# A two-layer graph network on one core: of every 64 gathered chunks, SyncE and ScalarE each load one row by row

## The reference

```python
def _gcn_conv(x, W, b, src, dst, n):
    h = x @ W
    deg = segment_sum(ones, dst)
    dinv = where(deg > 0, rsqrt(deg), 0)
    msgs = h[src] * (dinv[src] * dinv[dst])[:, None]
    return segment_sum(msgs, dst) + b

h = maximum(_layernorm(x), 0)
h = h @ W_pre + b_pre
h = relu(_gcn_conv(h, W1, b1, src + loops, dst + loops, n))
h = relu(_gcn_conv(h, W2, b2, src + loops, dst + loops, n))
x = x + (h @ W_post + b_post)
h = maximum(_layernorm(x), 0)
x = x + attention(h)
```

## Time and profile before

| | us |
|---|---|
| median of 3 runs | 4922.3 |
| lowest, highest run | 4919.2, 4923.6 |
| the profiled execution's own time | 4947.8 |
| its span, from the first to the last instruction | 4945.9 |
| POOL busy, share of the span | 62% |
| PE, PEld busy | 57%, 42% |
| DVE, ACT busy | 27%, 8% |

### The profile page before, as it was taken

How to read it: one execution, slowest core, us unless ns; L and a number is a source line. 1 busy time by engine, 2 the same in 40 slices (tenths; PEclk the granted TensorE clock), 3 DMA queues, 4 the chain that set the end, 5 groups by cost and what they waited for, 6 DMA issues and landing times.

```text
span 4945.9 us, 31104 instructions
## 1 busy us (share of the span) xinstructions
PE 2821.1 (57%) x10330; PEld 2094.8 (42%) x10330; DVE 1321.9 (27%) x3053; ACT 380.4 (8%) x1154; POOL 3056.4 (62%) x3240
## 2 busy tenths in 40 slices
PE   3266565665656656566635667655555555555543
PEld 2144444444434444444424446534344443443432
DVE  8211111121211112111112323223232232322345
ACT  2110000000000000000100000000000000000000
POOL 0466666666666666666366666666666666666552
PEclk8577676777767777677767766677676776766666
DMA  6433333333333333333233434344343443444334
GB/s 186 121 103 106 104 106 103 106 106 106 105 103 106 105 107 105 103 106 103 77 94 110 110 106 108 107 114 110 104 114 107 113 110 104 113 109 111 98 91 127
DMA packets 294666, 534.91 MB, mean 108 GB/s; under 512 B 76792, under 2 KB 194472, under 8 KB 294504
## 3 DMA queue, kind: packets, MB, share of 16 engines
q0 software_dynamic: 153184, 413.34, 31.3%
q1 hardware_dynamic: 141320, 119.55, 8.1%
HBM read 480.91 MB, written 51.74 MB: 108 GB/s over the span
## 4 chain that ended last, share of the span: by engine, by line
PE 37%; issue 30%; another core or an unknown queue 22%; DVE 10%; ACT 1%; POOL 0%; DMA 0%; DVEq 0%; ACTq 0%; POOLq 0%
PE ps L1098 26%; PE ps L937 3%; PE ps L1033 3%; PE ps L1034 2%; DVE acc L1655 2%; DVE sel L1482 1%; PE ps L931 1%; DVE xin L1491 1%; DVE sel L1346 1%; DVE acc L1510 1%; DVE xin L1336 1%; DVE tsb L1508 0%; DVE stats L1512 0%; PE ps L1061 0%
## 5 line engine op out<-in xcount | busy, mean ns | idle before, releaser
L633 POOL DMA_INDIRECT big<-tab,idx x3126 | 2955.9, 946 | 1721.2 <-issue 1067.2
L1098 PE MATMUL ps<-big,sel 128*128 128x257 f32 (+1 forms) x6252 | 2084.5, 463 | 1112.8 <-issue 1093.0
L1098 PEld LDWEIGHTS ps<-big,sel 128*128 128x128 f32 x6252 | 1405.7, 232 | 1644.2 <-issue 1456.6
L1655 DVE SCALAR_TENSOR_TENSOR acc<-ps,here,acc 128x257 f32<-128x257 f32 (+1 forms) x392 | 190.1, 485 | 3417.6 <-remote 2934.0
L1482 DVE TENSOR_TENSOR sel<-rel,ps 128x1024 f32<-128x1024 f32 x392 | 474.4, 1211 | 0.0
L1033 PE MATMUL ps<-xin,Wc 128*128 128x128 f32 x784 | 167.8, 313 | 186.9 <-issue 183.9
L1033 PEld LDWEIGHTS ps<-xin,Wc 128*128 128x128 f32 x784 | 133.5, 211 | 207.6 <-issue 190.1
L937 PE MATMUL ps<-Wp,xin 128*128 128x256 f32 x392 | 132.0, 469 | 106.7 <-DVEq L1511 84.3
L1655 DVE SCALAR_TENSOR_TENSOR acc<-ps,beyond,acc 128x257 f32<-128x257 f32 (+1 forms) x392 | 186.6, 476 | 0.0
L1034 PE MATMUL ps<-xin,bc_row 1*128 1x128 f32 x392 | 113.9, 352 | 124.0 <-issue 123.6
L931 PE MATMUL ps<-ident,xin 128*128 128x128 f32 x392 | 95.7, 319 | 94.9 <-issue 82.8
(11 more groups left out here) (182 smaller groups left out, 1364.0 us busy)
## 6 DMA issues: line engine op xcount, KB each, us to landing
big<-tab,idx POOLq DMA_INDIRECT x3126
tab<-big SPq DMA_DIRECT2D x14, 910.0 KB, 5.5
acc<-tab SPq DMA_DIRECT2D x98, 130.0 KB
tab<-tsb SPq DMA_DIRECT2D x98, 128.0 KB
acc<-tab SPq DMA_DIRECT2D x98, 128.0 KB
xres<-acc SPq DMA_DIRECT2D x98, 128.0 KB
xin<-in_x_dram SPq DMA_DIRECT2D x97, 128.0 KB
big<-in_x_dram SPq DMA_DIRECT2D x13, 896.0 KB, 8.5
```

The costliest lines, as they stand in the source:

```text
L633: return pool.indirect_dma_start(out=to, out_offset=None, in_=table, in_offset=bass.IndirectOffsetOnAxis(ap=index, axis=0))
L1098: ins = pe.matmul(sums[H % SUMS][:, 0:n_c], sel[:, H % RING * CPH + j, :], G[:, H % PORTIONS * CPG + j, 0:n_c], start=(j == 0), stop=(j == ...
L1655: dve.scalar_tensor_tensor(out=row(T, wide), in0=sums[H % SUMS][:, 0:wide], scalar=mask[:, n:n + 1], in1=row(T, wide), op0=ALU.mult, op1=A ...
```

## The change

Every eighth half (n = 8k + 7, for k from 1 to 23 in each layer, `piece(n)` gives k) has its last two chunks, j = 6 and 7, loaded without a gather. SP loads the rows of chunk 6, ScalarE those of chunk 7, each row with a DMA of its own, into `hrow`, which has two places for each of the two. Four tiles share the 128 rows of a piece, so each engine issues 32 in a tile (`share`). SP first loads the piece's edge sources into `hidx` (`next_indices`); VectorE multiplies them by the row's bytes (`row_offsets` of VectorE, one instruction a piece), and each engine reads 32 of the products at once into registers. TensorE waits before each of the two chunks until the piece's loads have landed (`fed`), and takes the chunk from `hrow`.

```diff
+PERIOD = 4
...
+        hrow = sb("hrow", [P, 2, 2, W])
+        hidx = sb("hidx", [1, 3, 2, P], I32)
...
+        PIECES = FULL // (PERIOD * CPI) - 1
+        def piece(n):
+            k = (n + 1) // (2 * PERIOD) - 1
+            return k if (n + 1) % (2 * PERIOD) == 0 and 1 <= k <= PIECES else 0
+        def feeder(n, j):
+            return j - (CPG - 2) if piece(n) and j >= CPG - 2 else None
...
+        def share(m):
+            return m * P // PERIOD, (m + 1) * P // PERIOD
...
+            def row_loads(c, t):
+                k, m = t // PERIOD + 1, t % PERIOD
+                K = k + c * PIECES
+                if k > PIECES:
+                    return
+                if m == 0:
+                    n = c * HALVES + (k - 1) * 2 * PERIOD
+                    if n:
+                        sp.wait_ge(g_agg, n)
+                    next_indices(c, k)
+                    sp.wait_ge(h_off, K)
+                lo, hi = share(m)
+                _, at = nc.values_load_multi_w_load_instructions(
+                    hidx[0:1, K % 3, 0, lo:hi], engines=[mybir.EngineType.SP], min_val=0, max_val=(N - 1) * 4 * width(c),
+                    skip_runtime_bounds_check_because="indices of edges are node numbers")
+                for e in range(lo, hi):
+                    sp.dma_start(hrow[e:e + 1, K % 2, 0, 0:width(c)].bitcast(U8),
+                                 offset_of(at[e - lo], tab2 if c else tab1, width(c))).then_inc(hs_in[K % 2], 16)
...
                     if t >= 2:
                         store_tab2(t - 2)
+                    row_loads(0, t)
...
                         sp.wait_ge(c2_h, t + 1)
                         load_self(1, t + AR)
+                    row_loads(1, t)
...
                         for j in range(min(CPG, C - n * CPG)):
+                            if feeder(n, j) is not None:
+                                continue
                             gather(G[:, s * CPG + j, 0:width(c)], table, idx[:, n * CPG + j:n * CPG + j + 1]).then_inc(g_in[s], 16)
...
                 for i in range(ITERS - 3):
+                    at = row_offsets(0, i)
+                    row_loads(0, i, at, 0, 4)
                     for n in (2 * i, 2 * i + 1):
                         selT_copy(n, 0)
...
                     if due(i - 3):
                         root(i - 3)
+                    at = row_offsets(1, i)
+                    row_loads(1, i, at, 0, 3)
                     if due(i - 5):
                         values_out(i - 5)
                     if due(i - 4):
                         normed_turned(i - 4)
+                    row_loads(1, i, at, 3, 4)
...
+                x_j = G[:, H % PORTIONS * CPG + j, 0:n_c]
+                k, feed = piece(n), feeder(n, j)
+                K = k + c * PIECES
+                if feed == 0:
+                    pe.wait_ge(hs_in[K % 2], fed(c, k))
+                if feed == 1:
+                    pe.wait_ge(ha_in[K % 2], fed(c, k))
+                if feed is not None:
+                    x_j = hrow[:, K % 2, feed, 0:n_c]
...
+                    dve.wait_ge(h_idx, 32 * K)
+                    dve.tensor_scalar(hidx[:, K % 3, :, :], hidx[:, K % 3, :, :], 4 * width(c or k == PIECES), None, ALU.mult)\
+                       .then_inc(h_off, 1)
```

More of the change, by code:

```diff
@@ L16 @@
 I32 = mybir.dt.int32
+U8 = mybir.dt.uint8
 ALU = mybir.AluOpType
@@ L295, in build_gnn @@
         g_sel = sem("g_sel")
+        h_idx = sem("h_idx")
+        h_off = sem("h_off")
+        hs_in = [sem("hs_in0"), sem("hs_in1")]
+        ha_in = [sem("ha_in0"), sem("ha_in1")]
         a_in = [sem(f"a_in{s}") for s in range(AR)]
@@ L358, in build_gnn, with first_edge, fed, offset_of @@
         whole = FULL // P * P
+        PIECES = FULL // (PERIOD * CPI) - 1
+        assert (N - 1) * 4 * W < 1 << 24 and PIECES * PERIOD + 2 < ITERS - 3
+        def piece(n):
[3 more added lines that the diff above has]
+            return j - (CPG - 2) if piece(n) and j >= CPG - 2 else None
+        def first_edge(k, feed):
+            return ((k + 1) * PERIOD * CPI - 2 + feed) * P
+        def fed(c, k):
+            K = k + c * PIECES
+            return 16 * P * ((K + 1) // 2)
+        def share(m):
+            return m * P // PERIOD, (m + 1) * P // PERIOD
+        def offset_of(at, table, n):
+            return table.rearrange("n w -> (n w)").bitcast(U8)[bass.ds(at, 4 * n)].rearrange("(a b) -> a b", a=1)
         def landed(H):
-            return 16 * sum(min(CPG, C - n % HALVES * CPG) for n in range(H % PORTIONS, H + 1, PORTIONS))
+            return 16 * sum(min(CPG, C - n % HALVES * CPG) - 2 * (piece(n % HALVES) > 0)
+                            for n in range(H % PORTIONS, H + 1, PORTIONS))
         def cols(t):
@@ L506, in load_self, with next_indices @@
                 sp.dma_start(row(T, width(c)), (tab2 if c else tab1)[cols(t), :]).then_inc(a_in[s], 16)
+            def next_indices(c, k):
+                K = k + c * PIECES + 1
+                if K <= 2 * PIECES:
+                    for feed in range(2):
+                        at = first_edge((K - 1) % PIECES + 1, feed)
+                        sp.dma_start(hidx[0:1, K % 3, feed, :], src[at:at + P].rearrange("(a e) -> a e", a=1)).then_inc(h_idx, 16)
+            def row_loads(c, t):
[16 more added lines that the diff above has]
+                                 offset_of(at[e - lo], tab2 if c else tab1, width(c))).then_inc(hs_in[K % 2], 16)
             for s in range(XB):
@@ L510, in _ @@
             with sp.If(bad == 0):
+                next_indices(0, 0)
                 for t in range(AR):
@@ L828, in general_attention, with row_offsets, row_loads @@
                     exps(BATCHES - 2 + q)
+            def row_offsets(c, i):
+                k, m = (i - 1) // PERIOD + 1, (i - 1) % PERIOD
+                K = k + c * PIECES
+                if not 1 <= k <= PIECES:
+                    return ()
+                if m == 0:
+                    n = c * HALVES + (k - 1) * 2 * PERIOD
+                    if n:
+                        act.wait_ge(g_agg, n)
+                    if c and k == 1:
+                        for s in range(2):
+                            act.wait_ge(c1_w[s], 16 * (TILES // 2 + 1))
+                    act.wait_ge(h_off, K)
+                lo, hi = share(m)
+                _, at = nc.values_load_multi_w_load_instructions(
+                    hidx[0:1, K % 3, 1, lo:hi], engines=[mybir.EngineType.Activation], min_val=0, max_val=(N - 1) * 4 * width(c),
+                    skip_runtime_bounds_check_because="indices of edges are node numbers")
+                return at
+            def row_loads(c, i, at, first, end):
+                k, m = (i - 1) // PERIOD + 1, (i - 1) % PERIOD
+                K = k + c * PIECES
+                for q in range(first * len(at) // 4, end * len(at) // 4):
+                    e = share(m)[0] + q
+                    act.dma_start(hrow[e:e + 1, K % 2, 1, 0:width(c)].bitcast(U8),
+                                  offset_of(at[q], tab2 if c else tab1, width(c))).then_inc(ha_in[K % 2], 16)
             bad = act.value_load(flag_i[0:1, 0:1], min_val=0, max_val=1)
@@ L1097, in chunk @@
                     return
-                ins = pe.matmul(sums[H % SUMS][:, 0:n_c], sel[:, H % RING * CPH + j, :], G[:, H % PORTIONS * CPG + j, 0:n_c],
+                x_j = G[:, H % PORTIONS * CPG + j, 0:n_c]
+                k, feed = piece(n), feeder(n, j)
+                K = k + c * PIECES
+                if feed == 0:
[4 more added lines that the diff above has]
+                    x_j = hrow[:, K % 2, feed, 0:n_c]
+                ins = pe.matmul(sums[H % SUMS][:, 0:n_c], sel[:, H % RING * CPH + j, :], x_j,
                                 start=(j == 0), stop=(j == last))
@@ L1484, in select, with row_offsets @@
                                   iota_p.unsqueeze(1).to_broadcast([P, CPH, P]), ALU.is_equal).then_inc(g_sel, 1)
+            def row_offsets(c, i):
+                k = i // PERIOD
+                K = k + c * PIECES + 1
+                if i % PERIOD == 0 and k <= PIECES and K <= 2 * PIECES and (k or not c):
+                    dve.wait_ge(h_idx, 32 * K)
+                    dve.tensor_scalar(hidx[:, K % 3, :, :], hidx[:, K % 3, :, :], 4 * width(c or k == PIECES), None, ALU.mult)\
+                       .then_inc(h_off, 1)
             def rows(c, t, b, before):
```

2 lines of the change are left out of this document (added).

## The result

The changed kernel takes 6302.2 us (median; 6295.6 to 6315.5), beside 4922.9 us for the kernel before, measured beside it: 1.281 times as long, with a 95% interval of 1.279 to 1.282. The forecast was 5029 us, with a range up to 5290. It is slower, as forecast, but by 1380 us and not by 107. The profiled execution took 6295.6 us.

A forecast was written before the change was run, and what follows sets the result against it. POOL's own time was 30.0 of each 34.3 us cycle, TensorE's bursts deciding its restart. Layer 1 gaining 57 and layer 2 losing 165 gave +107 us: 5029 us for the median, range 4800 to 5290.

The forecast's parts named there:

- p: Price of a one-row DMA on SP or ScalarE: taken as 0.30 us, bounds 0.27 and 0.47.
- T + 32p = 10.6 us a tile: Time SP or ScalarE spends per tile on one register read and 32 row loads; taken as covered in layer 1.
- T: One read of 32 registers on SP or ScalarE: taken as 1.0 us, between 0.5 and 2.0.
- B: Rival: SP and ScalarE become the bound at 22.8 us a tile, 24.4 with ScalarE's work; 5675 us, chance 0.07.
- The gathers removed: On POOL, both layers: 92 gathers fewer at 1.25 us each save 115 us.
- rival C: Landing of gathers, not POOL's issue, sets the 1.43 us a chunk, so no gain: 4922 us, chance 0.05.
- Layer 1 gains 57: In layer 1 the row loads are hidden and the removed gathers make the layer 57 us shorter.
- SP's store ahead of the rows in layer 2: SP's last row loads stand behind store_l in their tile of use: 222 us lost, layer 2 net 165 longer.
- A: Rival: all row loading is hidden and only the removed gathers count; 4807 us, or 4791 with waits, chance 0.28.
- What costs nothing: VectorE's 46 multiplications, the DMA engines' at most 376,832 packets, and the waits for h_off and g_agg were taken as free.
- D: Layer 2, from the even half's end to the odd one's: 8.8 + 2T + 56p = 27.6 us, against 8.6 before.
- the three places of POOL's cycle: Where the even half ends after POOL's restart: at 0, 3.0 or 11.7 us, losing 16.2, 7.7 or 5.0; 9.6 a piece.

The follow-up runs named there:

- a layer without rows: Changed kernel with no row loads, register reads or waits for them: 4793.5 us on a slow-paced chip, 4156.3 us on a quick one, ratio 0.974 on both.
- the rows first: Changed kernel with SP's row loads ahead of store_l and load_self in layer 2: 5893.0 us slow-paced (1.197), 4154.9 us quick (0.973).
- experiment 3: Changed kernel with one line moved, so SP loads rows before store_l and load_self in layer 2: 4154.9 and 4154.8 us on quick chips, ratio 0.973.
- rows loaded for nobody: Changed kernel with all gathers made and used again, the rows still loaded but TensorE not waiting for them: 4267.4 us on a quick chip, ratio 0.9995.
- The fixed rows: Changed kernel with each row DMA from a fixed row, no register read or MOVE: 4226.5 and 4228.7 us quick, 5238.2 us slow-paced (1.064).
- the share of 64 half rows: Changed kernel with each row loaded by two DMAs of half a row, and semaphores for each layer: 6597.0 us on a quick chip, ratio 1.545.

## Why the prediction was wrong

**Where the 1380 us lie**, by the windows. Against 2159 us a layer without rows, layer 1 loses 533 us and layer 2 loses 524 with the rows first (2692, 2683): that is the price of the shares. SP's order in layer 2 adds 3082 - 2683 = 399. The gathers give back 129. The sum is 1327. Of the 53 us that are missing, 34 lie between and behind the layers; the rest is about the precision of a sum over several chips and executions.

**What failed is the price of a row**, p = 0.30 with bounds of 0.27 and 0.47, and the T + 32p = 10.6 us a tile that follows, and with them the step that such a tile is covered by POOL's 22.8 us in layer 1. Measured on SP in layer 1 were 24.2/32 = 0.76 us a row and 24.2 + 2.1 = 26.3 us a tile; from one share to the next it was 28.5 us on average. The price was taken from L395, issued before POOL gathers at all, and from medians. A median over a nearly idle queue says little about a full one where the pace depends on what else runs. The trace had a sign of it twice: L506 had a maximum of 1478 ns beside its median of 378, and TensorE executed eight matmul records in 16 us without a wait, which I read as TensorE's affair. Such stretches cost SP nothing while it issued at most four DMAs a tile; with 65 instructions a share they made SP the bound. Why the instructions are slow in them stays open.

**Which rival it was.** B by its mechanism, the issuing engines become the bound: it asked for 22.8 us a tile with the register read and a layer 1 that grows, and got 26.3 us and a layer 1 464 us longer. TensorE's waits in layer 1, which the forecast excluded, are there too. B was priced at p = 0.65 for a wrong reason, a register operation a row, and given 0.07; the MOVE is there and takes 29 ns at the quick pace. Its 5675 us fell short of the 6302 as well: it had 150 us for layer 1.

**Steps that held.** *The gathers removed:* 115 us forecast, 112 and 129 measured on the two kinds, so rival C is out. The saved issue time on POOL was worth its whole length. The Trainium skill ("DMA: Bandwidth & Descriptors", Issuing engines are not separate DMA queues) calls such a saving usually small; here it was the whole gain. *Layer 1 gains 57:* exactly so on the quick kind, against +464 on the slow-paced. *SP's store ahead of the rows in layer 2:* the place was right and the move of one line shows it; it costs layer 2 291 us on the quick kind and 399 on the slow-paced, where the forecast had 222. *A*, all hidden, is what the order of experiment 3 makes of it on the quick kind, not what the change as written does. *What costs nothing:* rows loaded for nobody cost nothing on the quick kind. The DMA engines had far less to do than the bound of 376,832 packets: part 3 of the pages counts 23,736 more than before on the queues of SP and ScalarE.

**What only seems to fit** is the loss of layer 2 on the quick kind, 291/23 = 12.7 us a piece where the forecast had 9.6. Two errors meet in it. D was 27.6 us in the forecast and 41.0 measured (49.8 on the slow-paced chip). With T = 2.1 and p = 0.33 the forecast's own terms give only 8.8 + 4.2 + 18.5 = 31.5; in the piece shown the root comes 10.3 us behind the even half's end instead of 4.3, and `load_self` 3.7 us behind `store_l` instead of 0.4. But more of D was covered, too: 41.0 - 12.7 = 28 us and not 18, as the three places of POOL's cycle gave, a cycle that the quick kind hasn't got. The fixed rows there say the same: D is 34.8 us and layer 2 loses 58/23 = 2.5 us a piece. And TensorE's waits in layer 2 were some 26 to 35 us long on both kinds, where the forecast looked for 10 to 20.

**The register read T** was 2.1 us where 1.0 was taken. An estimate from the 200 ns a register of the Trainium skill ("Runtime: NRT & Kernel Launch", Instruction fetch mechanics) would have been 6.4. The trace doesn't agree with it for these 32 registers, read from SBUF in one instruction: they took 66 ns each.

## What to carry to other kernels

Price an instruction from rows in the very stretch in which it will be issued, and look at the maximum of a group beside its median before many are put on a queue that was nearly idle. In a program written out by hand, count behind which waits a load stands: one line moved was worth 322 us here on a quick chip. And measure on more than one chip, since what gained 2.7% on one lost 20% on another.

## What was not expected of the hardware

- The same program took 4267 to 4269 us on four chips and 4922 to 4945 us on at least two others. POOL's gathers keep their pace on both (1.25 us), and so do the DMA engines: a packet of q1 takes 0.094 x 16 x 4266.8/141,320 = 45 ns on the quick kind, as in the earlier trace rows. What differs in the traces is how fast SP, ScalarE and TensorE carry out instructions in stretches in which POOL gathers. From part 3 of the page, the kernel before on a quick chip:

```profile
q1 hardware_dynamic: 141320, 119.55, 9.4%
```

- On the slow-paced kind a share issued in a pause of POOL is as quick as on the other (10.7 us), and one beside its gathers takes 24 to 33 us in the piece shown. That the gathers cause it is an inference from such timelines; no run separates them. The Trainium skill ("Runtime: NRT & Kernel Launch", Instruction fetch mechanics) holds the fetch of instructions to be hidden behind their issue; no run here shows whether the fetch is what is slow. The changed kernel's packets of the queue `q14 instruction` took 0.43 us on average on the slow-paced chip and 0.37 on the quick one, so they themselves are hardly slower.
- A row DMA whose address is in a register costs one MOVE of 29 ns more than one with a fixed address; a constant added to that address costs a further operation, and the share of 64 half rows came to 23.9 us.
